# Second layer's weighted expert sums taken into the loop of its shared units, with ScalarE scaling rows and three loads in flight

## The reference

```
def _L1_ffn_ref(x, ...):                      # x: 8 x 512 tokens, 128 features
    xn = layernorm(x)
    probs = softmax(xn @ gate_w.T)
    tk_probs, tk_idx = top_k(probs, 2)
    tk_probs = tk_probs / (sum(tk_probs) + 1e-05)
    out = swiglu(x, sWg, sWu, sWd)            # one shared expert, all tokens
    for e in range(8):
        out = out + w[:, e] * swiglu(x, Wg[e], Wu[e], Wd[e])   # w holds tk_probs
    return out
x = x + _L1_ffn_ref(layernorm(x), ...)
```

## Time and profile before

| what | us |
|---|---|
| median of 3 runs (lowest to highest) | 1148.78 (1146.61 to 1149.73) |
| the profiled execution: its own time | 1151.23 |
| the profiled execution: span of the instructions | 1149.5 |
| busy: TensorE, VectorE, ScalarE, GpSimd | 900.5, 843.4, 758.9, 711.5 |

### The profile page before, as it was taken

How to read it: one execution, slowest core, us unless ns; L and a number is a source line. 1 busy time by engine, 2 the same in 40 slices (tenths; PEclk the granted TensorE clock), 3 DMA queues, 4 the chain that set the end, 5 groups by cost and what they waited for, 6 DMA issues and landing times.

```text
span 1149.5 us, 16137 instructions
## 1 busy us (share of the span) xinstructions
PE 900.5 (78%) x4818; PEld 684.7 (60%) x4818; DVE 843.4 (73%) x1510; ACT 758.9 (66%) x1507; POOL 711.5 (62%) x536
## 2 busy tenths in 40 slices
PE   1999487787787787877666999995778857999980
PEld 0764266666565565666565777773455646777760
DVE  6424589899999999945747777764677657888866
ACT  2347688888888788833424888884656635787870
POOL 1130299898998999960777544427764564477750
PEclk9996599999999999868967999996887857999995
DMA  4000586765777567700112577612110114455316
GB/s 113 5 10 5 136 199 211 218 176 173 247 192 186 193 209 209 175 19 1 47 54 86 131 202 204 184 61 66 52 37 32 38 45 123 139 170 159 111 45 182
DMA packets 127880, 139.21 MB, mean 121 GB/s; under 512 B 16054, under 2 KB 86181, under 8 KB 127796
## 3 DMA queue, kind: packets, MB, share of 16 engines
q1 hardware_dynamic: 117892, 121.15, 37.8%
q0 software_dynamic: 9088, 16.94, 4.6%
q10 hardware_dynamic: 816, 0.11, 0.1%
HBM read 76.86 MB, written 63.11 MB: 122 GB/s over the span
## 4 chain that ended last, share of the span: by engine, by line
PE 54%; DVE 16%; ACT 14%; POOL 7%; issue 6%; DMA 2%; DVEq 0%; SPq 0%; ACTq 0%; POOLq 0%; PEldq 0%
PE ps L1617 10%; PE ps L1618 9%; PE ps L1619 9%; DVE arena L1253 7%; POOL arena L615 5%; PE ps L1705 3%; PE ps L1675 3%; PE ps L1890 3%; ACT arena L828 2%; PE ps L1849 2%; ACT arena L818 2%; PE ps L1713 2%; DVE x L1516 2%; PE ps L1664 2%; ACT arena L817 2%
## 5 line engine op out<-in xcount | busy, mean ns | idle before, releaser
L615 POOL TENSOR_TENSOR arena<-arena 128x1024 f32<-128x1024 f32 x128 | 298.9, 2361 | 34.5 <-DVE arena L1253 30.8
L1253 DVE TENSOR_TENSOR_SCAN arena<-arena,ps 128x1024 f32<-128x1024 f32 x128 | 284.9, 2270 | 21.8 <-PE ps L1705 13.9
L640 POOL DMA_INDIRECT xs<-hx,slot x128 | 127.6, 997 | 100.7 <-DVE slot L1331 64.0
L1675 PE MATMUL ps<-ident,arena 128*128 128x128 f32 x1088 | 148.4, 287 | 20.4 <-POOL arena L615 17.5
L1675 PEld LDWEIGHTS ps<-ident,arena 128*128 128x128 f32 x1088 | 130.7, 148 | 27.8 <-POOL arena L615 23.8
L828 ACT ACTIVATE arena<-arena,bT 128x256 f32<-128x256 f32 x344 | 145.4, 494 | 0.0
L1705 PE MATMUL ps<-ident,arena 128*128 128x128 f32 x688 | 101.6, 295 | 53.7 <-DVE arena L1253 39.4
L1705 PEld LDWEIGHTS ps<-ident,arena 128*128 128x128 f32 x688 | 80.8, 150 | 96.2 <-ACT arena L828 79.1
L663 POOL DMA_INDIRECT yd<-yb,dest x92 | 94.6, 1028 | 53.6 <-ACT yb L935 31.3
L817 ACT ACTIVATE arena<-softplus_dt,Aneg 128x512 f32<-128x512 f32 x128 | 91.7, 716 | 40.1 <-DVE arena L1253 40.1
L1465 DVE TENSOR_TENSOR h_lo<-hs,h_hi 128x512 fp32r<-128x512 f32 x90 | 70.9, 801 | 43.9 <-ACT h_hi L914 43.6
(11 more groups left out here) (283 smaller groups left out, 2146.0 us busy)
## 6 DMA issues: line engine op xcount, KB each, us to landing
xs<-zero SPq DMA_DIRECT2D x16, 2340.0 KB, 11.6
arena<-bc_rows SPq DMA_DIRECT2D x64, 512.0 KB, 5.3
x_blk<-xs SPq DMA_DIRECT2D x52, 260.0 KB, 2.8
w_raw<-in_L_ffn_w SPq DMA_DIRECT2D x58, 128.0 KB
ys<-yb SPq DMA_DIRECT2D x29, 256.0 KB, 2.6
big<-yd SPq DMA_DIRECT2D x8, 512.0 KB, 3.5
w_raw<-in_L_ffn_Wg SPq DMA_DIRECT2D x23, 128.0 KB
w_raw<-in_L_ffn_Wu SPq DMA_DIRECT2D x23, 128.0 KB
```

Source lines behind the costliest of these rows:

```text
L615: nc.gpsimd.tensor_tensor(hc[M % 3], h[N % 3], row.unsqueeze(1).to_broadcast([P, NG, L]), ALU.mult)\
L640: pool.indirect_dma_start(out=xs, out_offset=bass.IndirectOffsetOnAxis(ap=slot[:, q, t:t + 1], axis=0), in_=hx[:, t, :], in_offset=None).t ...
L1253: nc.vector.tensor_tensor_scan(h[N % 3].rearrange("p g t -> p (g t)"), dA[N % 2].rearrange("p g t -> p (g t)"), ps[N % 2][:, :, :].rearran ...
L1675: return nc.tensor.matmul(out_, in_, ident[:, :], is_transpose=True, start=first_, stop=False, skip_group_check=True)
```

## The change

- `weigh(1)` is taken forward. ScalarE's two exps stand at the end of the attention stage, ahead of barrier 11, where the table of exp is loaded already. VectorE's five instructions stand behind `lay_out(1)`, ahead of the first `gate_h`. Barrier 12 and the table load behind it are gone.
- The sums are split. For an even batch ScalarE scales the second expert's rows in place (`weigh_outputs`, four instructions of 128 columns), VectorE scales and adds the first expert's as before (four), and adds the second's in one instruction of 512 columns. For an odd batch ScalarE scales both (eight instructions), and VectorE adds twice 512 columns. Over eight batches: 48 scalings on ScalarE; on VectorE 16 of the old instructions instead of 64, and 12 adds.
- The place of the sums: batches 0 to 3 are written into the loop over `U`, on ScalarE behind its work at `U` = 59, 60, 61 and 62, on VectorE behind its work at `U` = 60 to 63; batches 4 to 7 stand behind the loops.
- `load_outputs` has three semaphores; from batch 3 on it waits for the sums of batch b - 3, and the store of batch b - 3 is issued right behind the load of batch b.

```diff
+        gated, weighed = sem("gated"), sem("weighed")
+        FIRST_LOGITS, SECOND_LOGITS, SECOND_GATES = range(1, 4)
...
-        BARRIERS = (1, 3, 4, 7, 8, 11, 12)
+        BARRIERS = (1, 3, 4, 7, 8, 11)
...
+        LOADS_AHEAD = 3
+        SUMMED_WITHIN = 4
...
+        def by_scalar(b):
+            return range(2) if b % 2 else range(1, 2)
...
                 def load_outputs(b):
-                    if b >= 2:
-                        sp.wait_ge(combined, NB + b - 1)
+                    if b >= 3:
+                        sp.wait_ge(combined, NB + b - 2)
...
                 for b in range(NB):
                     load_outputs(b)
+                    if b >= LOADS_AHEAD:
+                        store_result(b - LOADS_AHEAD)
+                for b in range(NB - LOADS_AHEAD, NB):
+                    store_result(b)
...
@@ scalar, moe(k), in the loop over U @@
+                    if k and 0 <= U - units(k) + 3 < SUMMED_WITHIN:
+                        weigh_outputs(U - units(k) + 3)
+                if k:
+                    for b in range(SUMMED_WITHIN, NB):
+                        weigh_outputs(b)
...
+            def weigh_outputs(b):
+                if b == 0:
+                    act.wait_ge(gated, SECOND_GATES)
+                act.wait_ge(y_in[b % 3], 16 * (b // 3 + 1))
+                for q in by_scalar(b):
+                    for i in range(TPB):
+                        t = b * TPB + i
+                        last = nc.scalar.activation(yg[:, b, i, q, :], yg[:, b, i, q, :], ACT.Copy,
+                                                    scale=gate[:, q, t:t + 1])
+                last.then_inc(weighed, 1)
...
+            weigh(1)
             barrier(act, 11)
             moe(1)
-            barrier(act, 12)
-            nc.scalar.preload_act_table_set("natural_log_exp_and_others")
-            weigh(1)
...
@@ vector, moe(k) @@
                 lay_out(k)
+                if k:
+                    weigh(1, TOPK1_EPS)
...
+                    if k and 0 <= U - units(k) + 2 < SUMMED_WITHIN:
+                        combine(1, U - units(k) + 2)
+                if k:
+                    for b in range(SUMMED_WITHIN, NB):
+                        combine(1, b)
...
@@ vector, combine(k, b) @@
                 for q in range(2):
-                    for i in range(TPB):
+                    if k and q in by_scalar(b):
+                        dve.wait_ge(weighed, 2 + b + 1)
+                        last = nc.vector.tensor_tensor(x[:, w, :], x[:, w, :], yg[:, b, :, q, :], ALU.add)
+                    else:
+                        for i in range(TPB):
...
+            dve.sem_inc(gated, 1)
             take_counts(1)
             barrier(dve, 11)
             moe(1)
-            barrier(dve, 12)
-            weigh(1, TOPK1_EPS)
-            for b in range(NB):
-                combine(1, b)
```

More of the change, by code:

```diff
@@ L218, in mamba_moe_attention_moe_kernel @@
         po = sems("po", "z sz gated tr gc o add")
-        gt = [sems(f"gt{k}", "lt hot prefix slot cum table" + " back" * (1 - k) + " tk rz root" * k) for k in range(2)]
+        gt = [sems(f"gt{k}", "lt hot prefix slot cum table" + " tk rz root" * k) for k in range(2)]
         mo = [sems(f"mo{k}", "sent xt xh xl w h hi lo mm2 ye tr te " + " g sil um id wh" * k) for k in range(2)]
         combined = sem("combined")
-        gate_in, gate_exp = sem("gate_in"), sem("gate_exp")
+        gated, weighed = sem("gated"), sem("weighed")
+        FIRST_LOGITS, SECOND_LOGITS, SECOND_GATES = range(1, 4)
         blk_in = [sem(f"blk_in{i}") for i in range(3)]
@@ L226, in mamba_moe_attention_moe_kernel @@
         y_sent = [sem(f"y_sent{i}") for i in range(YSLOTS)]
-        y_in = [sem(f"y_in{i}") for i in range(2)]
+        y_in = [sem(f"y_in{i}") for i in range(3)]
         got = [sem(f"got{b}") for b in range(3)]
@@ L671, in fetch @@
             def fetch():
-                pool.wait_ge(gt[0]["back"], 1)
+                pool.wait_ge(gt[0]["table"], PLACES)
                 for i in range(NBLK[0], NBLK[0] + 3):
@@ L1412, in lay_out @@
                     link(nc.vector.tensor_reduce(off, moved, op=ALU.add, axis=AX.X))
-                    nc.vector.tensor_tensor(back[:, :, :], off, sm[:, 10:12, :], ALU.add).then_inc(s["back"], 1)
+                    nc.vector.tensor_tensor(back[:, :, :], off, sm[:, 10:12, :], ALU.add).then_inc(s["table"], 1)
             def weigh(k, eps):
@@ L1429, in weigh @@
                 link(nc.vector.reciprocal(gate[:, 0, :], t0))
-                link(nc.vector.tensor_tensor(gate[:, 1, :], gate[:, 0, :], top2, ALU.mult))
+                last = nc.vector.tensor_tensor(gate[:, 1, :], gate[:, 0, :], top2, ALU.mult)
+                if k:
+                    last.then_inc(gated, 1)
+                    dve.wait_ge(gated, SECOND_GATES)
+                else:
+                    link(last)
             def moe(k):
@@ L1511, in combine @@
                 else:
-                    dve.wait_ge(y_in[b % 2], 16 * (b // 2 + 1))
+                    dve.wait_ge(y_in[b % 3], 16 * (b // 3 + 1))
+                w = slice(b * TPB, (b + 1) * TPB)
                 for q in range(2):
-                    for i in range(TPB):
-                        t = b * TPB + i
-                        last = nc.vector.scalar_tensor_tensor(out=x[:, t, :], in0=yg[:, b, i, q, :],
-                                                              scalar=gate[:, q, t:t + 1], in1=x[:, t, :],
-                                                              op0=ALU.mult, op1=ALU.add)
+                    if k and q in by_scalar(b):
+                        dve.wait_ge(weighed, 2 + b + 1)
+                        last = nc.vector.tensor_tensor(x[:, w, :], x[:, w, :], yg[:, b, :, q, :], ALU.add)
+                    else:
+                        for i in range(TPB):
+                            t = b * TPB + i
+                            last = nc.vector.scalar_tensor_tensor(out=x[:, t, :], in0=yg[:, b, i, q, :],
+                                                                  scalar=gate[:, q, t:t + 1], in1=x[:, t, :],
+                                                                  op0=ALU.mult, op1=ALU.add)
                     if q == 0:
@@ L2004, in _ @@
             moe(1)
-            barrier(pe, 12)
 _IN_ORDER = ['L0_attn_x', 'L0_attn_ln_w', 'L0_attn_ln_b', 'L0_attn_in_proj_w', 'L0_attn_conv_w', 'L0_attn_conv_b',
```

23 lines of the change are left out of this document (11 added, 12 removed).

## The result

| kernel | median us (lowest to highest) | runs | ratio to before, 95% interval |
|---|---|---|---|
| before | 1150.61 (1146.57 to 1153.93) | 20 | |
| changed | 1146.03 (1143.30 to 1150.58) | 20 | 0.9965, 0.9952 to 0.9978 |

The change makes the kernel 4.6 us faster; 5.1 was forecast. The median of before, 1148.78 in the first three runs, came out at 1150.61 in twenty, and that is most of what lies between the forecast 1143.7 and the measured 1146.03.

The account below looks back on a forecast made before the run. VectorE with its loads was taken to bound the 30.6 us behind the last unit; a first load 0.5 late plus the chain of loads, scalings, held units and adds gave a 5.1 gain, 1148.78 to 1143.7, range 1141.6 to 1147.5.

Parts of the forecast that it names:

- The held units: Last units' silu, high half, low half, add and copy, queued behind the wait for the first load: 5 us in the path.
- steps 1 to 4: First load to batch 0 done: load 3.5, four scalings 1.3, held silu and high half, then VectorE's 3.05; done at 1122.8.
- Step 7: Last job behind eight scalings: `copy_y` 0.6, transposes at half clock 1.1, VectorE's add 0.7; 2.4 in all.
- The start: Start of the stage: gates taken ahead make the first load 0.5 late, bounds 0.1 and 0.9.
- step 9: Load 7, behind a store, near the end of the sums: 3.8 us, landing at 1136.8.
- Steps 5 and 9: Two loads waited for in full: load 3, after batch 0's sums, 3.5; load 7, behind a store, 3.8.
- The last store: End of the kernel: the last store, no longer piled up, lands in 2.6; bounds 2.6 and 3.9.
- hand-overs: Passing from one engine to the next along the end's chain: 0.06 each, sixteen put in as 1.0.
- rival A: Sums at the end: scalings at 0.39, loads 3 and 7 at 4.4; 1147.1, no difference that can be told; chance 0.14.
- Rival B: Start of stage: TensorE's gap delays the clock's rise; 5 us more gives 1146.2; chances 0.05 to no change, 0.04 over 1152.
- Rival C: Held units cost nothing, VectorE slipping their work between landings; 3 us less, 1140.7; chance 0.07.
- steps 3 and 4: Behind the first scalings: held silu 0.5 and high half 0.6, then VectorE's low half, adds and multiply-adds 3.05.

## Why the prediction was right

Its steps, each as time from the first load's issue:

| step | predicted | measured |
|---|---|---|
| counts' copy to first load, added | 0.5 | 0.53 |
| 1 first load there | 3.5 | 3.65 |
| 2 four scalings done | 4.8 | 4.9 |
| 3 held silu and high half done | 5.9 | 5.9 |
| 4 batch 0 done | 9.0 | 9.1 |
| 5 load 3 there | 12.5 | 13.15 |
| 6 eight scalings done | 15.0 | 15.6 |
| 7 last unit's add over | 17.4 | 17.7 |
| 8 batch 4 done | 19.2 | 19.5 |
| 9 load 7 there | 23.0 | 24.25 |
| 10 batch 7 done | 26.8 | 28.2 |
| 11 end of the span | 30.6 | 31.0 |

- **The held units (steps 1 to 4) came as forecast**: ScalarE idle for 7.07 until the first load, its scalings 0.295 apart (8 in 2.44, the value taken from L828), 1.2 GHz behind the wait. Running the units through (28.8 for 31.0) shows that this order is itself a cost; the prediction named the 5 us of held units but not that the kernel is better off without the place.
- **Step 7 came out right by another path, and that is luck**: 2.4 was put down for the copy, transposes at half clock (1.1) and the add, and 2.1 was measured. But TensorE's clock had risen again behind the held products (1.00 granted from 1126 to 1127, 2.4 GHz), the transposes took 0.66, and the add waited for VectorE itself, which had batch 3's two wide adds in front of it. The rows, TensorE's stretch first:

```profile
1126.00:1127.00 1.00, 0.26 (x2) 0.26 (x3) 0.73 (x2) 0.69 (x2) 0.00 (x0) 1.00 0.58 194
...
1126.74 0.66 PE L1929 MATMUL ps<-ident,ya 128*128 128x128 f32 x4 [1.97 <-ACT ya L942]
...
1126.31 1.42 DVE L1554 TENSOR_TENSOR x<-x,big 128x512 f32<-128x512 f32 x2 [0.27 <-ACT big L993]
1127.65 0.68 DVE L1512 TENSOR_TENSOR x<-x,ps 128x512 f32<-128x512 f32 x1
```

- **The start (0.5) came as forecast**: ScalarE's exps cost 0.2 where 0.1 was taken, and TensorE stood 0.62 where 0.7 was; 0.29 of these 0.82 were made up by the first load's issue. So VectorE's five instructions cost 0.34 in the end. The two runs that place them elsewhere show the mechanism: 1.5 where VectorE's list is full, nothing in its idle times.
- **The mis-sized term is that of a load behind a store (step 9)**: 3.8 was taken (half of 0.9 on top of 3.5 would have been 3.95); 4.7 was measured for load 7, and 4.0, 4.7, 4.0 and 5.1 for loads 3 to 6, which each have a store right ahead of them or behind. Load 7 had load 6 beside it as well, and the runs do not part the two: with the stores last, a load beside another took 4.4. Steps 5 and 9 together took 1.5 us more than was put down for them. The last store (2.3 for 2.6) and the hand-overs, for which 1.0 was put in as a lump at the end and which partly lay in the measured durations already, gave 1.0 back. That these nearly cancel is luck, too.
- **The gain was hit, the absolute time less well**: 1146.03 lies beyond the forecast's stretch (1141.8 to 1145.3) and in that of rival A, because the three runs of before from which it was reckoned were 1.8 below the median of twenty.
- **Rival A** fell in its first half (0.295, not 0.39) and held in its second: four of the five later loads took from 4.0 to 4.7 and one 5.1, with 4.4 as its figure for loads 3 and 7 (4.0 and 4.7). **Rival B did not occur**: the clock rose at the same place. The granted clock in the half microsecond that begins 8.56 us behind the counts' copy:

```profile
957.00:957.50 0.50, 0.21 (x1) 0.00 (x0) 0.50 (x2) 0.50 (x1) 0.50 (x1) 0.65 0.83 203
957.50:958.00 0.50, 0.37 (x2) 0.32 (x3) 0.50 (x2) 0.14 (x1) 0.50 (x1) 1.00 0.97 321
```

Before it was 0.59 in the half microsecond that began 8.38 behind that copy; from 957.5 on it is 2.4 GHz. TensorE's gap lies directly at the rise, so what a longer or an earlier one would do is not shown. **Rival C** is refuted by steps 3 and 4, which took the time forecast.

**Where the gain that one may expect on paper went.** The gates' 3.4 us were won and 0.5 paid for them. Of what the sums gained, the runs show which part gave and which took: the third load gave 9.3, without which the change is slower than before; the place took 2.2, and ScalarE's share, in that place, 3.5. These don't add up, since each was altered with the others in place. What stayed was the chain load, scalings, adds, next load. VectorE's saved work, 18.4 us to 12.7, could shorten nothing while VectorE waited for that chain. Once the loads were out of it, ScalarE's share did pay: VectorE alone, with eight loads and the gates at the end, needs 29.6. With the gates ahead its sums would begin 5.5 behind the first load's issue, as in the run of the gates alone, in place of 9.0; with 17.9 for the 64 and 2.7 to the end that is some 26.1 (an estimate, not run), and with ScalarE's share it is 22.4.

The Trainium skill (ScalarE: Activation LUTs, Rules for kernel authors) says that adds and multiplies belong on VectorE and not on ScalarE. These runs agree with it with three loads in flight (27.5 against 31.0, though a part of that is the held units). With eight, where VectorE alone would be the bound, 22.4 against the estimate of 26.1 speaks against it.

## What to carry to other kernels

An instruction that waits for a transfer, written ahead of other work in a list that is gone through strictly in turn, holds that work: move work "among" other work only where what it waits for has landed by then. Before an engine's work is cut at the end of a kernel, look whether a transfer waits for that work and that work for the transfer; here giving every load its own semaphore (it had its own buffer already) took 6.6 us off the end, and all of the change 5.2. And small instructions cost what they last or nothing, by whether the engine's list has a gap just there.

## What the runs showed of the hardware

- Loads of 512 KB in one queue overlap well: one at a time, or a few beside stores, they took 3.4 to 5.9 us each; eight at once, issued within 3.4 us, landed at most 9.4 to 11.2 us after their issue, so that 4.2 MB took at most some 14.6 us.
- A store of 256 KB landed 2.3 us after its issue when nothing else was under way, and about 4.4 to 5.5 between loads; the same store piled up with seven others took 3.7 to 4.8 before. So spreading stores out helps the last one, and the end of the kernel with it, most.
